# First mixture of experts on one core: activation on pairs of pieces, masks one unit later, normalization applied by ScalarE

## The chip, the cores and the metric

One core of a Trainium2 chip runs the whole kernel. The metric is the device time of one execution in microseconds (us); the profile of one execution is taken beside it. Five engines work in parallel, each through its own list of instructions in order: TensorE (PE, with its weight loads PEld), VectorE (DVE), ScalarE (ACT), GpSimd (POOL) and SyncE (SP, which here only issues transfers). They wait for one another through counting semaphores.

## The reference, cut to what matters

A decoder of two layers over 16 sequences of 128 tokens with 256 features. Each layer has two attentions (the first layer: a gated recurrence and a masked attention) and a mixture of experts, and after each of the six comes `x = layernorm(x + sublayer(x))`. The change touches the third of the six, the first mixture of experts: 8 experts of inner width 64, of which each token uses the best two by router score.

```python
x1 = ragged_dot(xb, w1b, gs); x3 = ragged_dot(xb, w3b, gs)      # bf16
h = silu(x1) * x3
routed = ragged_dot(h, w2b, gs)
out = sum over the token's two experts of score * routed
x = layernorm(x + out)
```

## The kernel before, in words

The phases are named A to F, one for each sublayer. Phase C is the first mixture of experts. It computes all 8 experts for all tokens (8 x 64 = 512 hidden features) and masks the hidden values for each of the two choices before the product with `w2`. A **unit** is two sequences (256 tokens), so there are NU = 8 units; the 512 hidden features are N0 = 4 **pieces** of 128. For each piece f of unit t:

1. PE `c_up` writes both products (w1 and w3, four matmuls) into one PSUM bank of 512 columns; there is one bank for each piece.
2. ACT `c_up` (L824) copies the bank as bf16 into `up0`.
3. ACT `c_exp` (L832), DVE `c_den` (L1262: plus one, and a cap), ACT `c_ln` (L838), ACT `c_sig` (L846) make the sigmoid as exp(-ln(1 + exp(-x))); DVE `c_act` (L1271) multiplies it with x, POOL `c_prod` (L627) with the other product.
4. PE `c_mask` (L1783, two matmuls) spreads the 0/1 choice of each token over the piece's lanes, for choice 0 and choice 1. There are two mask banks for the four pieces.
5. DVE `c_hid` (L1282) multiplies mask and product into `hid0`, 512 columns, and so frees the mask bank.

For each unit and each choice r, PE `c_down` (L1796, eight matmuls) sums the four pieces through `w2`, ACT `c_round` (L866) copies the result as bf16, DVE `c_sub` (L1293, called `add` in the pipeline) adds it, scaled by the token's score, to x. Then the layer norm: DVE `stats` (L1077 to L1083) gives mean and variance, POOL `inverse_root` (L597) the inverse root, DVE `apply` (L1090) writes the normalized rows into `X`.

Each engine's list is made by `pipelined(engine, n, stages)`: in **turn** s it emits, in the order of the list, each stage with its lag for unit s - lag. The order inside a turn is therefore fixed by hand, for each engine. `behind(f, k, stage)` gives the stage for the piece k places before f, in this turn or the one before. Buffers for exp, den, sig, act, prod and ln hold two pieces and are used in turn. Before the change the orders of turn s are (piece, and unit in brackets):

- PE: up0[s], mask2[s-1], down0[s-2], up1[s], mask3[s-1], down1[s-2], up2[s], mask0[s], up3[s], mask1[s]
- ACT: up0, ln3[s-1], exp0, sig3[s-1], up1, ln0, exp1, sig0, round[s-2], up2, ln1, exp2, sig1, up3, ln2, exp3, sig2 (unit s where nothing is said)
- DVE: den0, act3[s-1], hid2[s-1], den1, apply[s-3], act0, hid3[s-1], den2, act1, hid0, add[s-2], den3, act2, hid1, stats[s-2]
- POOL: inverse root[s-3], prod0, prod1, prod2, prod3

Behind phase C comes phase D, whose first step on PE, `xpose_unit` and `d_proj`, reads the rows of unit 0: PE transposes (L1737), ACT `evac_d` (L880), DVE `d_x_low` (L1312), then the matmuls of `d_proj` (L1606). ACT and DVE come to that work only when all of phase C in their lists is done. POOL then clears `kz` (L641, one memset of 4096 columns) and splits the keys.

Phase A already applies its norm on ACT: POOL makes `nmean` (L603) and `nbias` (L606), ACT writes the rows (L758).

Of the kernel before, what the change touches and what calls it, by code (L numbers as in the profile page):

```python
# [168 lines left out]
def decoder(nc, a, out, xg, yg, qk):  # L169
    with ExitStack() as ctx:  # L170
# [378 lines left out]
        def _(pool):  # L549
# [87 lines left out]
            pipelined(pool, NU, [(3, inverse_root("C"))] + [(0, c_prod(f)) for f in range(N0)])  # L637
# [77 lines left out]
        def _(act):  # L715
# [111 lines left out]
            def c_exp(f):  # L827
                def step(t, slot):
                    act.wait_ge(sem("C_up"), t * N0 + f + 1)
                    if f >= 2 or not (isinstance(t, int) and t < 1):  # L830
                        act.wait_ge(sem("C_den"), t * N0 + f - 1)
                    sc.activation(exp0[:, f % 2, :], up0[:, f, 0, :], ACT.Exp, scale=-1.0).then_inc(sem("C_exp"), 1)  # L832
                return step

            def c_ln(f):
                def step(t, slot):
                    act.wait_ge(sem("C_den"), t * N0 + f + 1)
                    sc.activation(ln0[:, f % 2, :], den0[:, f % 2, :], ACT.Ln).then_inc(sem("C_ln"), 1)  # L838
                return step

            def c_sig(f):
                def step(t, slot):
                    act.wait_ge(sem("C_ln"), t * N0 + f + 1)
                    if f >= 2 or not (isinstance(t, int) and t < 1):
                        act.wait_ge(sem("C_act"), t * N0 + f - 1)
                    sc.activation(sig0[:, f % 2, :], ln0[:, f % 2, :], ACT.Exp, scale=-1.0).then_inc(sem("C_sig"), 1)  # L846
# [3 lines left out]
            c_up(0)(0, 0)  # L850
            c_exp(0)(0, 0)
            route_exp()

# [13 lines left out]
            stages = []  # L867
            for f in range(N0):
                up, exp = (c_up(f), c_exp(f)) if f else (but_first(c_up(f)), but_first(c_exp(f)))
                stages += [(0, up), behind(f, 1, c_ln, N0), (0, exp), behind(f, 1, c_sig, N0)]  # L870
                if f == 1:
# [1242 lines left out]
```

## Time and profile before

| | us |
|---|---|
| time, median of 3 runs (lowest to highest) | 812.95 (812.26 to 814.93) |
| time of the profiled execution | 808.24 |
| its span | 806.5 |
| phase C, first `c_den` to the first matmul of `d_proj` | 178.44 to 262.37 |

In the page, busy time is the time an engine's instructions took, and the mean granted clock of PE (PEclk, 1.00 is 2.4 GHz, 0.50 is 1.2 GHz) stands beside each stretch. Behind an instruction in the timeline, square brackets say how long its engine was idle before it and what ended that. Start times count from the span's start. A duration is not the distance to the next start: on ACT and DVE the next instruction begins somewhat before the last one has ended.

### The profile page before, as it was taken

What the parts mean: (1) busy time and instruction counts of PE and PEld (TensorE: products, weight loads), DVE (VectorE), ACT (ScalarE), POOL (GpSimd) and SP (SyncE); (2) the same over time, 40 slices, a digit from 0 to 9 for tenths busy, and PEclk for the clock granted to TensorE, in tenths of its full rate; (3) what the DMA queues carried; (4) which work ended last, traced back from release to release, by engine and by line L of the source; (5) the groups of instructions that cost most, each with busy time, mean ns of one, the idle gap of its engine ahead of it and who ended that gap; (6) DMA issues with size and microseconds to landing.
All of it is one profiled execution on the core that took longest, in us unless ns stands there. A gap on an engine that the chain in (4) does not pass through costs nothing.

```text
span 806.5 us, 17830 instructions
## 1 busy us (share of the span) xinstructions
PE 704.8 (87%) x5074; PEld 627.8 (78%) x5075; DVE 556.4 (69%) x1498; ACT 469.1 (58%) x1179; POOL 234.6 (29%) x399
## 2 busy tenths in 40 slices
PE   6887699958864988999999999999699989999972
PEld 5886477734432988999998999999599978888872
DVE  4786387757888446777786788887566765555376
ACT  4453466538782227777776788887345545555433
POOL 3122200033334600112121121111154515555544
PEclk9999699966695899999999999999699999999996
DMA  9940000000002586656667566652025433333162
GB/s 291 355 118 0 1 1 1 0 0 1 0 1 105 154 278 203 179 162 202 190 189 207 146 192 168 160 157 74 0 84 136 144 95 98 97 99 102 45 227 79
DMA packets 66486, 95.59 MB, mean 119 GB/s; under 512 B 11391, under 2 KB 52993, under 8 KB 66305
## 3 DMA queue, kind: packets, MB, share of 16 engines
q1 hardware_dynamic: 63024, 86.51, 36.3%
q0 software_dynamic: 3408, 8.43, 2.9%
q8 instruction: 26, 0.43, 0.2%
q14 instruction: 28, 0.22, 0.1%
HBM read 62.45 MB, written 33.36 MB: 119 GB/s over the span
## 4 chain that ended last, share of the span: by engine, by line
PE 58%; issue 16%; DVE 12%; DMA 4%; POOL 3%; ACT 3%; SPq 3%; DVEq 0%; POOLq 0%; ACTq 0%
PE bank L1875 13%; PE bank L1861 7%; PE bank L1951 6%; PE bank L2017 5%; PE bank L1850 4%; PE bank L1844 3%; PE bank L2041 3%; PE bank L1968 3%; PE bank L1606 3%; PE bank L1891 2%; PE bank L2005 2%; SPq L478 1%; DMA k_D<-stage_d 1%; DVE X L1090 1%; PE bank L1640 1%
## 5 line engine op out<-in xcount | busy, mean ns | idle before, releaser
L1875 PE MATMUL bank<-f_mem,late_mem 128*128 128x68 f32 (+3 forms) x1024 | 127.9, 268 | 0.0
L1875 PEld LDWEIGHTS bank<-f_mem,late_mem 128*128 128x128 f32 x1024 | 124.5, 192 | 0.7 <-issue 0.5
L597 POOL TENSOR_TENSOR rstd<-var,power 128x2 f32<-128x2 f32 (+1 forms) x64 | 41.7, 651 | 219.4 <-DVE var L1083 208.5
L1336 DVE TENSOR_REDUCE smax<-bank 128x4 f32<-128x512 f32 x128 | 88.2, 690 | 22.3 <-PE bank L1850 20.9
L915 ACT ACTIVATE late_mem<-bank 128x512 f32<-128x512 f32 x128 | 77.7, 607 | 21.6 <-PE bank L1861 19.3
L905 ACT ACTIVATE late_mem<-bank,smax 128x128 f32<-128x128 f32 x256 | 73.8, 384 | 11.4 <-DVE smax L1336 11.4
L1861 PE MATMUL bank<-ident,late_mem 128*128 128x128 f32 x512 | 77.3, 273 | 2.9 <-ACT late_mem L905 1.6
L1850 PE MATMUL bank<-kz,qs 128*128 128x256 f32 x256 | 75.1, 376 | 0.0
L1861 PEld LDWEIGHTS bank<-ident,late_mem 128*128 128x128 f32 x512 | 59.2, 141 | 3.6 <-ACT late_mem L905 2.0
L899 ACT ACTIVATE late_mem<-late_mem 128x512 f32<-128x512 f32 x64 | 41.0, 641 | 24.1 <-DVE late_mem L1343 23.3
L1850 PEld LDWEIGHTS bank<-kz,qs 128*128 128x128 f32 x256 | 48.7, 191 | 6.1 <-issue 0.3
L1951 PE MATMUL bank<-x_hi,w_hi 128*128 128x256 f32 x176 | 51.6, 293 | 1.0 <-DVE x_lo L1400 1.0
L1951 PE MATMUL bank<-x_lo,w_hi 128*128 128x256 f32 x176 | 50.8, 288 | 0.0
L1951 PE MATMUL bank<-x_hi,w_lo 128*128 128x256 f32 x176 | 50.7, 288 | 0.0
L1844 PE MATMUL bank<-causal,identb 128*128 128x512 bf16 x128 | 48.7, 381 | 1.2 <-DVE hidden_mem L1327 1.2
L1343 DVE TENSOR_TENSOR late_mem<-bank,smax 128x512 f32<-128x512 f32 x64 | 44.3, 692 | 6.9 <-DVE smax L1336 0.5
L686 POOL DMA_INDIRECT xg<-X,idx x32 | 33.6, 1049 | 42.7 <-DMA xg<-X,idx 21.2
L698 POOL DMA_INDIRECT yg<-attn_w,dest x39 | 38.8, 995 | 20.4 <-issue 12.0
L1968 PE MATMUL bank<-w_hi,hid_hi 128*128 128x256 f32 (+1 forms) x96 | 29.9, 311 | 13.8 <-DVE hid_lo L1417 13.7
L977 ACT ACTIVATE f_mem<-bank 128x256 f32<-128x256 f32 x40 | 15.3, 384 | 40.9 <-PE bank L1951 40.7
L1407 DVE TENSOR_TENSOR f_mem<-bank,f_mem 128x256 f32<-128x256 f32 x40 | 17.0, 424 | 30.0 <-ACT f_mem L977 29.7
L627 POOL TENSOR_TENSOR late_mem<-late_mem,f_mem 128x256 bf16<-128x256 bf16 x32 | 21.4, 669 | 52.1 <-DVE late_mem L1271 52.1
(285 smaller groups left out, 2069.9 us busy)
## 6 DMA issues: line engine op xcount, KB each, us to landing
qs<-q_D SPq DMA_DIRECT2D x64, 128.0 KB, 2.7
kz<-k_D SPq DMA_DIRECT2D x128, 64.0 KB, 2.6
qs<-q_E SPq DMA_DIRECT2D x64, 128.0 KB, 2.7
kz<-k_E SPq DMA_DIRECT2D x128, 64.0 KB, 2.5
xg<-f_mem SPq DMA_DIRECT2D x1, 5031.0 KB, 22.7
late_mem<-xg SPq DMA_DIRECT2D x39, 129.0 KB, 2.1
q_D<-stage_d SPq DMA_DIRECT2D x8, 512.0 KB, 2.9
k_D<-stage_d SPq DMA_DIRECT2D x8, 512.0 KB, 4.0
```

Source lines behind the costliest of these rows:

```text
L597: gp.tensor_tensor(rstd[:, slot, 0:n], var[:, slot, 0:n], power[:, 0:n], ALU.pow).then_inc(sem("ln_rstd"), 1)
L899: sc.activation(sp[:, g, :, :], sp[:, g, :, :], ACT.Exp).then_inc(sem("core_exp"), 1)
L905: ins = sc.activation(sp[:, g, i, :], bank[g][:, i * P:(i + 1) * P], ACT.Exp, bias=smax[:, g, i:i + 1])
L915: sc.activation(spt[:, g, :, :], bank[4 + g % 2][:, :], ACT.Copy).then_inc(sem("core_pts"), 1)
L1336: ve.tensor_reduce(smax[:, g, :], v, axis=AX.X, op=ALU.max, negate=g not in SUBS).then_inc(sem("core_max"), 1)
L1343: ve.tensor_tensor(sp[:, g, :, :], v, smax[:, g, :].unsqueeze(2).to_broadcast([P, HG, P]), ALU.subtract).then_inc(sem("core_sub"), 1)
L1844: mm(bank[g][:, :], identb[:, :], causal[:, :].unsqueeze(1).to_broadcast([P, HG, P]), start=True, stop=False)
L1850: ins = mm(bank[g][:, i * D:(i + 1) * D], qs[slot][:, a_ * P:(a_ + 1) * P], kz[:, slot, :, a_ * P:(a_ + 1) * P], start=False, stop=(i == 1))
L1861: ins = nc.tensor.transpose(bank[4 + g % 2][:, i * P:(i + 1) * P], sp[:, g, i, :], ident[:, :])
L1875: ins = mm(bank[6][:, h * (DH + 1):to * (DH + 1)], spt[:, g, i, :], vf[:, slot, h:to, :].rearrange("p h d -> p (h d)"), start=True, stop=True)
L1951: ins = mm(bank[r][:, m * UT:(m + 1) * UT], w[:, lo:lo + P], x[:, t % 2, k, :], start=(n == 1), stop=(n == 3 * KC))
L1968: ins = mm(halves(6 + t % 2)[:, j, :], h[lanes, r, cols], v[lanes, w], start=(f == n == j == 0), stop=(f == NF - 1 and n == 2 and j == UB ...
```

## The change

Exp, den, ln, sig, act and prod work on a **pair** of pieces (512 columns) in place of one (256 columns): NP0 = 2 instructions of each for a unit in place of 4, with buffers of twice the size for both pairs. The masks move: PE makes all four in the turn after the unit's up products, and DVE's four `hid` follow there. The statistics move one turn later. `apply` leaves DVE: POOL gets `nmean` and `nbias` in phase C too, ACT writes the rows. The orders of turn s become (a number behind exp, den, ln, sig, act, prod is now a pair):

- PE: up0[s], mask0[s-1], down0[s-2], up1[s], mask1[s-1], down1[s-2], up2[s], mask2[s-1], up3[s], mask3[s-1]
- ACT: up0, up1, ln1[s-1], exp0, sig1[s-1], round[s-2], up2, up3, ln0, exp1, sig0, apply[s-3]
- DVE: hid0[s-1], den0, act1[s-1], hid1[s-1], stats[s-3], den1, act0, hid2[s-1], hid3[s-1], add[s-2]
- POOL: prod1[s-1], inverse root[s-3], shift[s-3], prod0

```diff
@@ POOL
-            def c_prod(f):
+            def shift(phase, base):
+                def step(t, slot):
+                    gp.tensor_tensor(nmean[:, slot, :], mv[:, slot, :, 0], minus[:, 0:UB], ALU.mult).then_inc(sem("A_minus"), 1)
+                    pool.wait_ge(sem("A_minus"), t + 1 + base)
+                    pool.wait_ge(sem("ln_rstd"), t + 1 + LN[phase])
+                    gp.tensor_tensor(nbias[:, slot, :], nmean[:, slot, :], rstd[:, slot, :], ALU.mult
+                                     ).then_inc(sem("A_shift"), 1)
+                return step
+            def c_prod(p):
                 def step(t, slot):
-                    pool.wait_ge(sem("C_act"), t * N0 + f + 1)
-                    if f >= 2 or not (isinstance(t, int) and t < 1):
-                        pool.wait_ge(sem("C_hid"), t * N0 + f - 1)
-                    gp.tensor_tensor(prod0[:, f % 2, :], act0[:, f % 2, :], up0[:, f, 1, :], ALU.mult
+                    pool.wait_ge(sem("C_act"), t * NP0 + p + 1)
+                    if not (isinstance(t, int) and t < 1):
+                        pool.wait_ge(sem("C_hid"), (t - 1) * N0 + 2 * p + 2)
+                    gp.tensor_tensor(prod0[:, p, :, :], act0[:, p, :, :], up0[:, 2 * p:2 * p + 2, 1, :], ALU.mult
                                      ).then_inc(sem("C_prod"), 1)
-            pipelined(pool, NU, [(3, inverse_root("C"))] + [(0, c_prod(f)) for f in range(N0)])
+            pipelined(pool, NU, [(1, c_prod(1)), (3, inverse_root("C")), (3, shift("C", NU)), (0, c_prod(0))])
@@ ACT
                 def step(t, slot):
                     act.wait_ge(sem("C_hx"), t * N0 + f + 1)
                     if not (isinstance(t, int) and t < 1):
-                        act.wait_ge(sem("C_prod"), (t - 1) * N0 + f + 1)
+                        act.wait_ge(sem("C_prod"), (t - 1) * NP0 + f // 2 + 1)
                     sc.activation(up0[:, f, :, :], halves(HB[f]), ACT.Copy).then_inc(sem("C_up"), 1)
+            def c_apply(t, slot):
+                act.wait_ge(sem("A_shift"), t + 1 + NU)
+                for j in range(UB):
+                    ins = sc.activation(xrow(t * UB + j), y[:, slot, j, :], ACT.Identity,
+                                        bias=nbias[:, slot, j:j + 1], scale=rstd[:, slot, j:j + 1])
+                ins.then_inc(sem("ln_x"), 1)
+            pipelined(act, NU, [(0, but_first(c_up(0))), (0, but_first(c_up(1))), (1, c_ln(1)), (0, but_first(c_exp(0))),
+                                (1, c_sig(1)), (2, c_round), (0, c_up(2)), (0, c_up(3)), (0, c_ln(0)), (0, c_exp(1)),
+                                (0, c_sig(0)), (3, c_apply)])
@@ DVE
-            add, stats, apply = layer_norm("C", c_sub, own_n=2 * UB, split=True)
+            add, stats, _ = layer_norm("C", c_sub, own_n=2 * UB, split=True)
+            pipelined(dve, NU, [(1, c_hid(0)), (0, c_den(0)), (1, c_act(1)), (1, c_hid(1)), (3, stats),
+                                (0, c_den(1)), (0, c_act(0)), (1, c_hid(2)), (1, c_hid(3)), (2, add)])
@@ PE, c_up
                     if not isinstance(t, int):
-                        pe.wait_ge(sem("C_hid"), t * N0 + f - 3)
+                        pe.wait_ge(sem("C_hid"), t * N0 + f - N0 - 1)
@@ PE
-                stages += [(0, c_up(f)), behind(f, 2, c_mask, N0)]
+                stages += [(0, c_up(f)), (1, c_mask(f))]
                 if f < 2:
                     stages.append((2, c_down(f)))
```

`c_down(r)` for unit t keeps its wait for all four `hid` of its unit, `C_hid` at (t + 1) * 4.

## Rows read from the trace of the kernel before

**Rows 1.** The page, part 1: busy time of each engine over the whole span.
```profile
PE 704.8 (87%) x5074; PEld 627.8 (78%) x5075; DVE 556.4 (69%) x1498; ACT 469.1 (58%) x1179; POOL 234.6 (29%) x399
```

**Rows 2.** Windows of phase C: busy time by engine, PEclk, DMA share, GB/s.
```profile
182.00:252.00 70.00, 55.79 (x296) 29.34 (x296) 56.00 (x173) 50.91 (x131) 24.41 (x38) 0.72 0.00 1
208.00:218.00 10.00, 9.47 (x41) 4.63 (x42) 8.08 (x26) 7.36 (x19) 3.33 (x6) 0.50 0.00 0
```

**Rows 3.** Waits in phase C, 175 to 256: us in total, times, longest.
```profile
DVE f_mem L1262 <- ACT f_mem L832: 9.1, 15, 2.0
PE bank L1767 <- DVE hidden_mem L1282: 8.6, 10, 1.7
```

**Rows 4.** Timeline of ACT: the copy of piece 0 of units 2 and 7.
```profile
188.19 0.60 ACT L824 ACTIVATE f_mem<-bank 128x512 bf16<-128x512 f32 x1
...
234.02 0.59 ACT L824 ACTIVATE f_mem<-bank 128x512 bf16<-128x512 f32 x1
```

**Rows 5.** Timeline of ACT: a copy of 512 columns and two functions of 256.
```profile
208.99 0.60 ACT L824 ACTIVATE f_mem<-bank 128x512 bf16<-128x512 f32 x1 [0.87 <-PE bank L1767]
209.48 0.41 ACT L838 ACTIVATE late_mem<-f_mem 128x256 f32<-128x256 bf16 x1
209.79 0.41 ACT L832 ACTIVATE f_mem<-f_mem 128x256 bf16<-128x256 bf16 x1
```

**Rows 6.** Timeline of DVE: act, hid and the beginning of an add.
```profile
240.68 0.29 DVE L1271 TENSOR_TENSOR late_mem<-f_mem,late_mem 128x256 bf16<-128x256 bf16 x1
240.89 0.68 DVE L1282 TENSOR_TENSOR hidden_mem<-bank,late_mem 128x512 bf16<-128x512 f32 x1
241.49 0.91 DVE L1293 SCALAR_TENSOR_TENSOR y<-hidden_mem,m,X 128x256 f32<-128x256 bf16 x2
```

**Rows 7.** Timeline of PE: a down and an up behind it, at either clock.
```profile
200.59 1.05 PE L1796 MATMUL bank<-late_mem,hidden_mem 128*128 128x256 bf16 x8
201.47 0.60 PE L1767 MATMUL bank<-up_mem,late_mem 128*128 x4
...
209.42 1.89 PE L1796 MATMUL bank<-late_mem,hidden_mem 128*128 128x256 bf16 x8
211.09 1.06 PE L1767 MATMUL bank<-up_mem,late_mem 128*128 x4
```

**Rows 8.** Groups by line and shape, whole span: busy us, mean ns | idle before.
```profile
L899 ACT ACTIVATE late_mem<-late_mem 128x512 f32<-128x512 f32 x64 | 41.0, 641 | 24.1 <-DVE late_mem L1343 23.3
...
L758 ACT ACTIVATE X<-y,nbias,rstd 128x256 f32<-128x256 f32 x8 | 4.3, 590 | 10.7 <-POOL nbias L606 10.7
...
L627 POOL TENSOR_TENSOR late_mem<-late_mem,f_mem 128x256 bf16<-128x256 bf16 x32 | 21.4, 669 | 52.1 <-DVE late_mem L1271 52.1
...
L706 POOL TENSOR_TENSOR ctx_mem<-ctx_mem,late_mem 128x512 f32<-128x512 f32 x6 | 8.1, 1351 | 7.4 <-DMA late_mem<-yg 7.4
...
L606 POOL TENSOR_TENSOR nbias<-nmean,rstd 128x2 f32<-128x2 f32 x8 | 1.6, 197 | 0.6
```

**Rows 9.** Timeline of DVE: the first den of phase C.
```profile
178.44 0.20 DVE L1262 TENSOR_SCALAR f_mem<-f_mem 128x256 bf16<-128x256 bf16 x1
```

**Rows 10.** Timeline of the end of phase C: DVE, POOL and PE.
```profile
248.04 0.68 DVE L1282 TENSOR_TENSOR hidden_mem<-bank,late_mem 128x512 bf16<-128x512 f32 x1
...
254.98 0.75 DVE L1077 BATCH_NORM_STATS2 st<-y 128x6 f32<-128x256 f32 x2
...
256.05 0.17 DVE L1083 TENSOR_SCALAR var<-mv 128x2 f32<-128x2 f32 x1
256.30 0.69 POOL L597 TENSOR_TENSOR rstd<-var,power 128x2 f32<-128x2 f32 x1 [3.83 <-DVE var L1083]
256.93 3.51 POOL L641 MEMSET kz<- 128x4096 f32 x1
257.03 4.60 DVE L1090 TENSOR_SCALAR X<-y,mv,rstd 128x256 f32<-128x256 f32 x2 [0.81 <-POOL rstd L597]
...
262.37 0.55 PE L1606 MATMUL bank<-xp_hi,wd_hi 128*128 128x256 f32 x1 [7.32 <-DVE xp_lo L1312]
```

More of the change, by code:

```diff
@@ L40 @@
 N0 = E * F0 // P
+NP0 = N0 // 2
 NF = 6
@@ L338, in decoder @@
         up0 = part(small_mem, 0, [P, N0, 2, UT], BF16)
-        exp0, den0 = (part(small_mem, (4 + k) * UT, [P, 2, UT], BF16) for k in range(2))
-        sig0, act0, prod0 = (part(late_mem, 2048 + k * UT, [P, 2, UT], BF16) for k in range(3))
+        exp0, den0 = (part(f_mem, 2112 + k * 2 * UT, [P, 2, 2, UT], BF16) for k in range(2))
+        sig0, act0 = (part(late_mem, 2048 + k * 2 * UT, [P, 2, 2, UT], BF16) for k in range(2))
+        prod0 = part(late_mem, 6400, [P, 2, 2, UT], BF16)
         xt1 = part(small_mem, 4 * KC * P, [P, 2, KC, P])
-        ln0 = part(late_mem, 2048 + 3 * UT, [P, 2, UT])
+        ln0 = part(early_mem, 0, [P, 2, 2, UT])
         qs = (rounded("qs0", "late_mem", 6400, [P, NP * P]), rounded("qs1", "f_mem", 3136, [P, NP * P]))
@@ L822, in step, with c_exp @@
                     if not (isinstance(t, int) and t < 1):
-                        act.wait_ge(sem("C_prod"), (t - 1) * N0 + f + 1)
+                        act.wait_ge(sem("C_prod"), (t - 1) * NP0 + f // 2 + 1)
                     sc.activation(up0[:, f, :, :], halves(HB[f]), ACT.Copy).then_inc(sem("C_up"), 1)
                 return step
-            def c_exp(f):
+            def c_exp(p):
                 def step(t, slot):
[L829 to L832, printed above, removed]
+                    act.wait_ge(sem("C_up"), t * N0 + 2 * p + 2)
+                    if not (isinstance(t, int) and t < 1):
+                        act.wait_ge(sem("C_den"), (t - 1) * NP0 + p + 1)
+                    sc.activation(exp0[:, p, :, :], up0[:, 2 * p:2 * p + 2, 0, :], ACT.Exp, scale=-1.0).then_inc(sem("C_exp"), 1)
@@ L833, in c_exp, with c_ln, c_sig @@
                 return step
-            def c_ln(f):
+            def c_ln(p):
                 def step(t, slot):
-                    act.wait_ge(sem("C_den"), t * N0 + f + 1)
-                    sc.activation(ln0[:, f % 2, :], den0[:, f % 2, :], ACT.Ln).then_inc(sem("C_ln"), 1)
+                    act.wait_ge(sem("C_den"), t * NP0 + p + 1)
+                    sc.activation(ln0[:, p, :, :], den0[:, p, :, :], ACT.Ln).then_inc(sem("C_ln"), 1)
                 return step
-            def c_sig(f):
+            def c_sig(p):
@@ L842, in step @@
                 def step(t, slot):
[L843 to L846, printed above, removed]
+                    act.wait_ge(sem("C_ln"), t * NP0 + p + 1)
+                    if not (isinstance(t, int) and t < 1):
+                        act.wait_ge(sem("C_act"), (t - 1) * NP0 + p + 1)
@@ L847, in c_sig @@
+                    sc.activation(sig0[:, p, :, :], ln0[:, p, :, :], ACT.Exp, scale=-1.0).then_inc(sem("C_sig"), 1)
                 return step
             sc.preload_act_table_set("natural_log_exp_and_others")
-            c_up(0)(0, 0)
-            c_exp(0)(0, 0)
-            route_exp()
             def but_first(step):
@@ L858, in but_first @@
                 return other
+            for f in range(2):
+                c_up(f)(0, 0)
+            c_exp(0)(0, 0)
+            route_exp()
             def c_round(t, slot):
@@ L866, in c_round @@
                     sc.activation(down0[:, slot, r, :], bank[4 + r][:, :], ACT.Copy).then_inc(sem("C_dnb"), 1)
[L867 to L871, printed above, removed]
-                    stages.append((2, c_round))
-            pipelined(act, NU, stages)
+            def c_apply(t, slot):
[7 more added lines that the diff above has]
+                                (0, c_sig(0)), (3, c_apply)])
             def evac_d(t, slot):
@@ L1074, in stats @@
                         add(t, slot)
+                    own.n, own.t = own_n, t
                     own.sync()
@@ L1287, in c_sub @@
             def c_sub(t, slot, own):
+                if not (isinstance(t, int) and t < 2):
+                    dve.wait_ge(sem("ln_x"), t - 1 + LN["C"])
                 for r, m in ((0, m1), (1, m2)):
@@ L1296, in c_sub @@
                         own.sync()
-            add, stats, apply = layer_norm("C", c_sub, own_n=2 * UB, split=True)
-            stages = []
-            for f in range(N0):
-                stages += [(0, c_den(f)), behind(f, 1, c_act, N0), behind(f, 2, c_hid, N0)]
-                if f in (2, 3):
-                    stages.append((2, add if f == 2 else stats))
-            stages.insert(4, (3, apply))
-            pipelined(dve, NU, stages)
+            add, stats, _ = layer_norm("C", c_sub, own_n=2 * UB, split=True)
+            pipelined(dve, NU, [(1, c_hid(0)), (0, c_den(0)), (1, c_act(1)), (1, c_hid(1)), (3, stats),
+                                (0, c_den(1)), (0, c_act(0)), (1, c_hid(2)), (1, c_hid(3)), (2, add)])
             def d_x_low(t, slot):
```

31 lines of the change are left out of this document (13 added, 18 removed).

## The prediction

> **What bounds the kernel now.** I read the page first: over the span PE is busy 87% [rows 1], but phase C is a tenth of the span and is judged by its own rows. The windows of its middle show no full engine: in 70 us PE has 55.8 busy, DVE 56.0, ACT 50.9, POOL 24.4 [rows 2]. PE's figure depends on its clock: the mean granted clock is 0.72, so it stood at 2.4 GHz for some 44% of the time and at 1.2 GHz for the rest (0.5 + 0.5 x 0.44), and where it stood at 1.2 GHz throughout, PE was busy 9.47 of 10 us. Then the waits: DVE's den waits for ACT's exp 9.1 us in all, PE's up products wait for DVE's hid 8.6 us [rows 3]. So the phase is a ring of short waits between PE, ACT and DVE, and what counts is the longest path around that ring in one turn. The copy of piece 0 of units 2 and 7 gives the turn: (234.02 - 188.19) / 5 = 9.17 us [rows 4]. Last I read the end of the phase in the timeline: from the last hid (248.04 + 0.68) to the first matmul of phase D (262.37) pass 13.65 us [rows 10], and phase D, the same code before and after, hangs on that matmul. So the sum is made for one point: when does `d_proj` begin?
>
> **Prices of single instructions.** From start to start ACT takes 0.49 us for the copy of 512 columns and 0.31 for 256 columns (durations 0.60, 0.41) [rows 5]. An exp of 512 columns took 0.64 us (f32) against 0.41 for 256; I take 0.62, and 0.52 to the next start. Bounds: 0.60, as a copy, and 0.64 [rows 5, 8]. DVE's act of 256 columns takes 0.29 and 0.21 to the next start; a second 256 columns cost nothing at least and 0.29 at most, I take 0.13: hid, not packed, needs 0.68 for 512, and a fixed part is paid once. So 0.42, and 0.34 to the next start. Hid takes 0.68, next start after 0.60; an add takes twice 0.91 and a short wait, 1.92 in all [rows 6]. POOL's product takes 0.67 for 256 columns. For 512 it lies between 0.67 and 1.35 (the f32 tensor-tensor of 512); I take 1.20, near the upper row because that is the same operation on the same engine [rows 8]. Crossing from one engine to another costs 0.08 (256.22 to 256.30) and 0.04 (256.99 to 257.03) [rows 10]; I take 0.07.
>
> **Work of each engine.** ACT per turn: 12 x 0.31 = 3.7 becomes 6 x 0.52 = 3.12, and apply adds 2 x 0.49 = 0.98 (duration 0.59, [rows 8]): +0.4. DVE: 4 acts at 0.21 become 2 at 0.34 (-0.16), 4 dens become 2 (about -0.2), apply leaves (-0.7): about -1.0. POOL: 4 x 0.67 becomes 2 x 1.20 (-0.3) and nmean, nbias add 0.4. PE: the same 40 matmuls. None of this decides unless the ring lets it.
>
> **The ring after the change.** Three orders matter. DVE now makes hid3[s-2] near the end of turn s-1, behind act0[s-1], where it used to be done early. PE's down0[s-2] needs it and stands in front of up1[s]. And on ACT ln1[s-1], exp0[s] and sig1[s-1] stand behind the copy up1[s]. Behind sig1[s-1] come act1[s-1] and prod1[s-1], for which the copy up2[s] waits because it overwrites what the product reads; and ln0, exp1, sig0[s] stand behind that. DVE makes hid3[s-1] only behind act0[s], which waits for sig0[s]. That closes the ring, from sig0 to sig0 of the next unit, at 2.4 GHz:
>
> act0 0.34, hid2 0.60, hid3 0.68 = 1.62; down0 0.88 and up1 0.60 = 1.48 [rows 7]; ACT up1 0.49, ln1 0.52, exp0 0.52, sig1 0.62 = 2.15; act1 0.42 and prod1 1.20 = 1.62; ACT up2 0.49, up3 0.49, ln0 0.52, exp1 0.52, sig0 0.62 = 2.64; six crossings 0.42. Sum 9.93 us.
>
> At 1.2 GHz PE is not yet free when hid3 is there: up0 (0.86) and mask0 (0.43, four and two matmuls at 0.21) start when hid2 is done at 1.16, then down0 1.67 and up1 1.06 [rows 7] end at 5.18 in place of 3.24 or so: +1.92, a ring of 11.85. With the clock's present share, 0.44 x 9.93 + 0.56 x 11.85 = 11.0 us. Hidden in the ring are add (1.92), hid0, den0 and stats on DVE, round and apply on ACT, and the two small POOL operations: DVE is through with add, hid0 and den0 at 4.4, sig1 comes at 5.2 or later; ACT's round ends before prod1; apply ends at 1.1 and up0 has to wait for prod0 until 1.83 anyway. So the copy up0 has the apply in front of it for nothing.
>
> **Where it begins.** The first den starts at 178.44 [rows 9], for 512 columns about 0.29; ln0, exp1, sig0 behind it end at 180.46. Turn 1 has no down; its ring goes through both products: 1.83 (act0, prod0, three crossings) + 2.64 + 1.83 + 2.64 = 8.94. Six turns with downs follow: sig0 of unit 7 ends at 180.46 + 8.94 + 6 x 11.0 = 255.4.
>
> **The end.** From there DVE runs act0, hid2, hid3, add[5], hid0, act1, hid1, stats[5] (1.24, from 254.98 to 256.22), hid2, hid3 of unit 7: done after 7.6 [rows 10]. Add[6] and stats[6] last until 10.8; the two downs (3.6 us at 1.2 GHz) and the second rounding let the last add end at 13.0, the last variance at 14.3. Then POOL's three operations, 0.69 + 2 x 0.20 and crossings, 1.2; two applies 0.98, `evac_d` behind them in ACT's list 0.60, `d_x_low` 0.68 and two crossings: `d_proj` starts after 18.0. Measured from the last hid that is 10.4 us, against 13.65 before: this end is 3.2 us shorter. Most of that is one stall that goes: the last apply took 4.60 us for two instructions, because POOL's memset (256.93, 3.51 us) ran beside it [rows 10]. ACT's apply of phase A took 0.59 an instruction [rows 8].
>
> The Trainium skill, page "SBUF — State Buffer", section "SBUF: two separate sides", says that VectorE and GpSimd share a port pair as an exclusive lock while ScalarE has its own port; by that rule the stall is gone wholly, as in my sum, and the trace agrees with its 4.60 us.
>
> **Sum.** 255.4 + 18.0 = 273.4 against 262.37: +11.0 us, thus 819.3 against the profiled execution's 808.24, and 812.95 + 11.0 = 824.0 against the median, which lies 4.7 us above the profiled one. Break-even is a ring of (262.37 - 18.0 - 180.46 - 8.94) / 6 = 9.16 us.
>
> **Rivals.**
> 1. *PE stays at 2.4 GHz* where down0 and up1 run. Ring 9.93, end 17.7: 180.46 + 8.94 + 59.6 + 17.7 = 266.7, +4.3 us, 817.3. For it: the phase had long stretches at that level. Against it: PE will idle more, 40 matmuls in a longer turn.
> 2. *PE is at 1.2 GHz for each of them*: 6 x 11.85, +16, 829. For it: the pair comes right behind PE's longest idle time in the turn.
> 3. *Up1 is never late* (down0 passes early enough). The ring is that of turn 1, 8.94: 180.46 + 7 x 8.94 + 17.7 = 260.7, -1.6 us, no change that can be told. Against it: the wait for all four hid stands in the code.
> 4. *Faster: work, not the ring, sets the turn.* Fewer, longer instructions relieve DVE, the busiest engine beside PE at 8 us of 10 [rows 2], by 1.0 us a turn. 9.17 becomes 8.2: 6 x -1.0 and -3.2 at the end give -9, 804. It decides when the ring takes under 9.16, that is, if the long ring of waits found above is broken somewhere by 1.9 us. Against it: even without down0 in it, the ring is 8.94.
>
> Beside rival 4 stands a rule of the Trainium skill that speaks for the change: page "VectorE: DVE Perf Modes", section "Rules for kernel authors", tells to keep the number of operations small, since each pays a fixed cost. The trace agrees on the fixed cost (0.41 us for 256 columns, 0.64 for 512), but no row says that a saving on DVE shortens a turn here.
>
> **How the numbers follow.** Forecast, ring 10.3 to 11.6: 0.60. Rival 1: 0.12, rival 2: 0.10, rival 3: 0.08, rival 4: 0.10. A measurement here tells 0.3%, 2.4 us, from no change. Slower: 0.82, same 0.08, faster 0.10. If the product takes 0.67 the result is 0.53 x 7 = 3.7 us less, with 1.35 it is 1 us more; both stay inside the clock's bounds. The range leaves out rivals 3 and 4 and what lies beyond rival 2: 813.5 to 829.5.
>
> **What would show it.** ACT's copy of piece 0 should return every 10 to 12 us in units 2 to 7, and some 9 us in turn 1; ACT should wait for PE before up1 (1 to 3 us) and for POOL before up2 (0.5 to 1 us); PE should wait for DVE's hid before down0; DVE should be idle 3 us or more of a turn, waiting for exp and sig; the applies at 0.59 us, none near 4 us; 10 to 11 us from the last hid to `d_proj`; phase D and all behind it unchanged in length. A turn of 9 us or less, or up1 ready before ACT asks for it, would make the prediction wrong.

## The result, and the profile after

The changed kernel takes 830.02 us (median of 4 runs, 829.3 to 832.41) against 813.25 us (4 runs, 812.26 to 814.93): a ratio of 1.0209, 95% interval 1.0181 to 1.0237. It is 16.8 us slower where +11.0 was forecast, and lies 0.5 us beyond the upper end of the range. The direction and the ring of waits were right; what the low clock does to that ring was put too small.

First the page of the changed kernel, part 1. Against [rows 1] DVE is 12 us less busy, and PE 9 us more with the same number of matmuls.

```profile
PE 713.3 (86%) x5074; PEld 633.9 (76%) x5075; DVE 544.2 (66%) x1450; ACT 472.2 (57%) x1147; POOL 234.6 (28%) x399
```

Then the starts of ACT's sig of the first pair in the timeline, for units 0, 1 and 7. They give the turns: 8.82 us for turn 1, and (264.02 - 193.94) / 6 = 11.68 us for the six behind it (11.06, 11.67, 12.24, 11.74, 12.23, 11.14). Forecast were 8.94 and 11.0.

```profile
185.12 0.61 ACT L852 ACTIVATE late_mem<-late_mem 128x512 bf16<-128x512 f32 x1
...
193.94 0.63 ACT L852 ACTIVATE late_mem<-late_mem 128x512 bf16<-128x512 f32 x1
...
264.02 0.63 ACT L852 ACTIVATE late_mem<-late_mem 128x512 bf16<-128x512 f32 x1
```

The same starts in the kernel before (sig of piece 0, units 0, 1 and 7) give 5.58 us for turn 1 and (237.88 - 184.88) / 6 = 8.83 us for the six behind it:

```profile
179.30 0.40 ACT L846 ACTIVATE late_mem<-late_mem 128x256 bf16<-128x256 f32 x1
...
184.88 0.41 ACT L846 ACTIVATE late_mem<-late_mem 128x256 bf16<-128x256 f32 x1
...
237.88 0.40 ACT L846 ACTIVATE late_mem<-late_mem 128x256 bf16<-128x256 f32 x1
```

So of the changed kernel's longer phase C, 17.1 us lie in the six turns (70.1 less 53.0) and 3.2 us in turn 1, and the stretch behind the start of the last sig0 gives 5.8 us back (18.7 instead of 24.5).

The waits between 174 and 300 us (total, times, longest) name the ring. PE waits 19.2 us for hid ahead of the up products, against 8.6 in [rows 3], and 12.8 more ahead of the masks; DVE's den waits 34.4 for exp, against 9.1; ACT's copy waits for PE and, new, for POOL's product. (The changed kernel also lets DVE's add wait for ACT's apply of two units earlier; no row of these waits shows DVE held there.)

```profile
DVE f_mem L1273 <- ACT f_mem L838: 34.4, 15, 3.6
ACT f_mem L830 <- PE bank L1774: 23.1, 13, 2.5
PE bank L1774 <- DVE hidden_mem L1293: 19.2, 8, 4.1
...
PE bank L1790 <- DVE hidden_mem L1293: 12.8, 7, 4.1
ACT f_mem L830 <- POOL late_mem L633: 10.8, 9, 1.8
```

One turn in the timeline, from act0[4] to sig0[5], with the engine's idle time in brackets. It is the forecast ring, link by link:

```profile
217.33 0.43 DVE L1282 TENSOR_TENSOR late_mem<-f_mem,late_mem 128x512 bf16<-128x512 bf16 x1 [0.22 <-ACT late_mem L852]
217.68 1.28 DVE L1293 TENSOR_TENSOR hidden_mem<-bank,late_mem 128x512 bf16<-128x512 f32 x2
...
218.50 1.03 PE L1774 MATMUL bank<-up_mem,late_mem 128*128 x4 [3.57 <-DVE hidden_mem L1293]
...
219.47 0.60 PE L1790 MATMUL bank<-f_mem,hidden_mem 16*128 x2
...
220.00 1.89 PE L1803 MATMUL bank<-late_mem,hidden_mem 128*128 128x256 bf16 x8
...
221.68 1.06 PE L1774 MATMUL bank<-up_mem,late_mem 128*128 x4
...
222.78 0.60 ACT L830 ACTIVATE f_mem<-bank 128x512 bf16<-128x512 f32 x1 [2.51 <-PE bank L1774]
...
224.31 0.62 ACT L852 ACTIVATE late_mem<-late_mem 128x512 bf16<-128x512 f32 x1
...
225.05 0.42 DVE L1282 TENSOR_TENSOR late_mem<-f_mem,late_mem 128x512 bf16<-128x512 bf16 x1 [0.31 <-ACT late_mem L852]
...
225.65 1.15 POOL L633 TENSOR_TENSOR late_mem<-late_mem,f_mem 128x512 bf16<-128x512 bf16 x1 [6.66 <-DVE late_mem L1282]
...
226.90 1.08 ACT L830 ACTIVATE f_mem<-bank 128x512 bf16<-128x512 f32 x2 [1.00 <-POOL late_mem L633]
...
228.91 0.63 ACT L852 ACTIVATE late_mem<-late_mem 128x512 bf16<-128x512 f32 x1
```

The windows of this turn (length, PE, PEld, DVE, ACT, POOL busy, PEclk, DMA share, GB/s) show what the forecast had not seen. PE is wholly idle in 216 to 218, and up0, mask0, down0 and up1, which run from 218.5 to 222.7, all run at 0.50, the level of 1.2 GHz. The clock is back at 1.00 only when they are done, and stays there while ACT waits for POOL's product instead. (In the turn before this one it rose a little earlier, for up1 already, 0.68 us instead of 1.06; that turn took 11.67 us, this one 12.24.) The mean over 76 us of such turns is 0.75, higher than the 0.72 of [rows 2].

```profile
186.00:262.00 76.00, 47.79 (x256) 25.01 (x254) 38.83 (x101) 44.68 (x85) 20.29 (x26) 0.75 0.00 0
...
216.00:218.00 2.00, 0.00 (x0) 0.00 (x0) 0.96 (x3) 2.00 (x5) 0.37 (x3) 0.75 0.00 0
218.00:220.00 2.00, 1.50 (x6) 0.60 (x7) 1.97 (x5) 0.61 (x2) 0.99 (x1) 0.50 0.00 0
220.00:222.00 2.00, 2.00 (x11) 1.44 (x11) 1.26 (x3) 0.26 (x1) 0.00 (x0) 0.50 0.00 0
222.00:224.00 2.00, 2.00 (x11) 0.92 (x10) 0.00 (x0) 1.22 (x3) 0.00 (x0) 0.54 0.03 8
224.00:226.00 2.00, 1.30 (x11) 0.73 (x9) 1.25 (x4) 1.90 (x4) 0.35 (x1) 1.00 0.02 4
```

This is a turn of PE's loop, for units 3 to 6. The turns of units 2 and 7 are written out, and there up0 has no wait for hid and is done long before. What is left behind the idle time, mask0, down0 and up1, runs at the low level there too, and these turns took 11.06 and 11.14 us. Unit 7:

```profile
254.62 0.60 PE L1790 MATMUL bank<-f_mem,hidden_mem 16*128 16x256 bf16 x2 [3.04 <-DVE hidden_mem L1293]
255.22 1.89 PE L1803 MATMUL bank<-late_mem,hidden_mem 128*128 128x256 bf16 x8
256.90 1.06 PE L1774 MATMUL bank<-up_mem,late_mem 128*128 128x256 bf16 x4
```

Last the end of the phase in the timeline, to be held against [rows 10]. The last hid ends at 272.53 and `d_proj` starts at 282.75, 10.2 us later (forecast 10.4, before 13.65). POOL's memset still runs beside the last apply, but the apply is now ACT's and takes its usual 1.09 us for two instructions.

```profile
271.24 1.29 DVE L1293 TENSOR_TENSOR hidden_mem<-bank,late_mem 128x512 bf16<-128x512 f32 x2 [0.45 <-PE bank L1790]
...
280.20 3.51 POOL L647 MEMSET kz<- 128x4096 f32 x1
280.31 1.09 ACT L878 ACTIVATE X<-y,nbias,rstd 128x256 f32<-128x256 f32 x2 [2.29 <-POOL nbias L610]
...
282.75 0.55 PE L1613 MATMUL bank<-xp_hi,wd_hi 128*128 128x256 f32 x1 [3.89 <-DVE xp_lo L1319]
```

Phase C (first den, 183.76, to `d_proj`) is thus 98.99 us long against 83.93. This length is given for every run below, because what lies around it scatters by some us from one execution to the next. Each of the two kernels was profiled once more. The kernel before (e5):

> The kernel before once more, for a second profile: how far do the phases that nothing touches wander from one execution to the next? In the first pair of profiles the changed kernel's phase C is 15.1 us longer, but its first den starts 5.3 us later and all behind phase C takes 3.8 us longer. Theory: both are scatter of one execution (the profiled one of before was 4.7 us under its median); then this profile has its first den nearer 181 and phase C at 83 to 86 us. Rival: the untouched phases of the kernel before are always faster; then den starts at 178.4 again and the rest takes 544.

It took 814.88 us, with a phase C of 85.0. The changed kernel (e6):

> The changed kernel once more, for a second profile, as the run before. Theory, scatter: phase C 98 to 100 us again, the turns 11 to 12.3 us with up0, mask0, down0 and up1 at 1.2 GHz in each of PE's loop turns; the rest within 4 us of 548, in either direction. Rival: the low clock in front of down0 was chance in the first profile; then some turns are near 10 us here and phase C is under 95.

It took 829.41 us, with a phase C of 99.07 and turns within 0.05 us of the first profile's. So the change lengthens phase C by 14.6 us (99.03 less 84.47, the means of two profiles each) of the 16.8.

### The profile page after: what moved, and what is told of

The parts are those of the page before. It is cut to its first block, busy times and chain, and to the rows that moved or that the text cites. A ratio compares the mean times of both kernels' runs of the same rounds, so it can differ in the third digit from the quotient of the medians.

```text
span 830.7 us, 17676 instructions
## 1 busy us (share of the span) xinstructions
PE 713.3 (86%) x5074; PEld 633.9 (76%) x5075; DVE 544.2 (66%) x1450; ACT 472.2 (57%) x1147; POOL 234.6 (28%) x399
## 4 chain that ended last, share of the span: by engine, by line
PE 56%; issue 15%; DVE 12%; ACT 5%; DMA 4%; SPq 3%; POOL 3%; ACTq 0%; DVEq 0%; POOLq 0%
PE bank L1882 12%; PE bank L1868 6%; PE bank L2024 5%; PE bank L1958 5%; PE bank L1857 3%; PE bank L1613 3%; PE bank L2048 3%; PE bank L1851 3%; PE bank L1975 3%; PE bank L1803 2%; PE bank L1898 2%; SPq L480 2%; PE bank L1647 2%; PE bank L2012 2%; DMA k_D<-stage_d 1%
## 5 line engine op out<-in xcount | busy, mean ns | idle before, releaser
L915 ACT ACTIVATE late_mem<-bank,smax 128x128 f32<-128x128 f32 x256 | 73.5, 383 | 11.3 <-DVE smax L1343 11.3
L1774 PE MATMUL bank<-up_mem,late_mem 128*128 (+1 forms) x128 | 26.0, 347 | 20.1 <-DVE hidden_mem L1293 19.2
L633 POOL TENSOR_TENSOR late_mem<-late_mem,f_mem 128x512 bf16<-128x512 bf16 x16 | 18.4, 1152 | 68.6 <-DVE late_mem L1282 68.6
```

The costliest lines, as they stand in the source:

```text
L915: ins = sc.activation(sp[:, g, i, :], bank[g][:, i * P:(i + 1) * P], ACT.Exp, bias=smax[:, g, i:i + 1])
```

## The experiments

The turns, phase C and time, side by side. The ratio is that to the kernel before as it ran beside each kernel, with medians of 810.5 to 813.3 us, so kernels are compared by the ratio and not by the time:

| kernel | mean of the six turns behind turn 1 | phase C | time | ratio, 95% interval |
|---|---|---|---|---|
| before | 8.83, 9.01 | 83.9, 85.0 | 813.25 | 1 |
| changed kernel | 11.68 | 99.0 | 830.02 | 1.0209 (1.0181 to 1.0237) |
| e1 filler in the loop | 10.57 | 92.4 | 827.22 | 1.0212 (1.017 to 1.0254) |
| e12 filler in each turn | 10.43 | 91.4 | 822.43 | 1.0136 (1.011 to 1.0162) |
| e2 up1 ahead of down0 | 10.47 | 92.1 | 825.09 | 1.0178 (1.0126 to 1.0231) |
| e3 all ups first | 8.95 | 82.6 | 815.63 | 1.0046 (1.0019 to 1.0072) |
| e7 hid2, hid3 early | 9.06 | 82.4 | 813.24 | 1.0019 (0.9998 to 1.0041) |
| e11 the same, apply on DVE | 9.08 | 85.4 | 814.74 | 1.0025 (0.9997 to 1.0052) |
| e8 e3, products on DVE | 8.82 | 80.8 | 809.83 | 0.9981 (0.9955 to 1.0008) |
| e10 e8, last apply early | 8.63 | 76.7 | 806.97 | 0.9936 (0.9913 to 0.9959) |
| e4 before, apply on ACT | 9.59 | 84.6 | 813.3 | 1.0028 (1.0012 to 1.0044) |
| e9 before, memset late | 8.53 | 78.3 | 808.54 | 0.9955 (0.9932 to 0.9979) |

**Is it the clock of that stretch (e1, e12)?** The changed kernel with 20 matmuls more, which nothing reads, ahead of up0's wait in the turns that run as a loop, so that PE is busy where it was idle:

```diff
+                    if not isinstance(t, int) and f == 0:
+                        for _ in range(5):
...
+                                    mm(halves(HB[f])[:, o, :], w[:, c, f * P:(f + 1) * P], XTB[:, c, bass.ds(t * UT, UT)],
...
                     if not isinstance(t, int):
                         pe.wait_ge(sem("C_hid"), t * N0 + f - N0 - 1)
```

> The changed kernel, with PE's four matmuls of up0 repeated five more times (20 matmuls, same bank, same result) in front of up0's wait for hid, where PE idles 3.6 us in each turn of the loop. Theory, clock: the ring itself is 9.9 us at 2.4 GHz; the turns take 11.7 us because the idle time before down0 lets the clock fall and up0, mask0, down0, up1 run at 1.2 GHz. Then the clock holds, the four turns of PE's loop fall to 10.0 to 10.4 us, and the kernel gets faster by 5 to 7 us than the changed one, about 824, although it does more work. Rival, order alone: the turn is set by waits that do not depend on the clock; then nothing is gained, and the filler, 2.2 to 4.3 us in a gap of 3.6, leaves 830 or costs some us.

The filled turns took 10.07 to 10.55 us. The first and the last of the six, which the edit doesn't reach, stayed at 11.06 and 11.15. In the timeline the critical stretch now runs in 0.61, 1.05 and 0.60 us instead of 1.03, 1.89 and 1.06:

```profile
202.85 0.61 PE L1780 MATMUL bank<-up_mem,late_mem 128*128 x4 [1.70 <-DVE hidden_mem L1293]
...
203.72 1.05 PE L1809 MATMUL bank<-late_mem,hidden_mem 128*128 128x256 bf16 x8
...
204.60 0.60 PE L1780 MATMUL bank<-up_mem,late_mem 128*128 x4
```

and its windows show the full clock where the changed kernel had 0.50:

```profile
202.00:204.00 2.00, 1.15 (x9) 0.68 (x10) 2.00 (x5) 0.48 (x1) 1.15 (x1) 1.00 0.00 0
204.00:206.00 2.00, 2.00 (x18) 1.44 (x17) 1.67 (x4) 0.88 (x3) 0.00 (x0) 1.00 0.00 0
```

The filler does not keep the clock up throughout. In the next turn it fell while the filler itself ran, and was back at 1.00 for the critical stretch:

```profile
210.00:212.00 2.00, 2.00 (x11) 1.45 (x10) 0.45 (x2) 2.00 (x5) 0.72 (x3) 0.50 0.00 0
214.00:216.00 2.00, 2.00 (x18) 1.38 (x17) 1.74 (x4) 0.96 (x2) 0.00 (x0) 1.00 0.00 0
```

There the slowed filler took 4.02 us and held up0 back until 213.23, some 0.3 us behind the end of hid2; so what the filler gives back is, if anything, less than what the low clock costs.

Phase C shrank by 6.6 us. The whole kernel did not show it: 827 us where some 824 were expected, and a ratio of 1.0212 beside the changed kernel's 1.0209, with an interval of 3.4 us to either side. So the filler was put in every turn from unit 2 on (`if f == 0 and not (isinstance(t, int) and t < 2)`) and timed in six runs:

> The changed kernel with 20 matmuls that nothing reads ahead of up0 in every turn from unit 2 on, the turns written out at either end included. Theory (the clock of the stretch up0 to up1 is what lengthens the turns behind turn 1, and the time it gives back reaches the end of the kernel): turn 1 stays 8.8, all five following turns 10 to 10.6, phase C 90.5 to 92.5 us against 99.0, and the kernel 6 to 8 us faster than the changed kernel, a ratio to the kernel before of 1.011 to 1.014. Rival (the phases behind give the gain back, as four runs of the first filler kernel left possible): the same phase C, and a ratio of 1.018 or more.

Turns of 10.77, 10.07, 10.58, 10.34, 10.47 and 10.34, phase C 91.4, and a ratio of 1.0136, as expected. By the two ratios that is 5.9 us under the changed kernel, give or take 3 us; by phase C it is 7.6. In some of these turns up0 still began at the low level (0.65 to 0.95 us), but down0 and up1 ran at 1.05 and 0.60 in all. So the low clock of that stretch costs about 6 to 7.6 us. The rest of the loss is the ring itself.

**Is it down0 in front of up1 (e2, e3)?** PE's order becomes up0, up1, down0, mask0, mask1, down1, up2, mask2, up3, mask3, and up0 and up1 no longer wait for hid:

```diff
-                    if not isinstance(t, int):
+                    if not isinstance(t, int) and f >= 2:
                         pe.wait_ge(sem("C_hid"), t * N0 + f - N0 - 1)
...
-                stages += [(0, c_up(f)), (1, c_mask(f))]
+            pipelined(pe, NU, [(0, c_up(0)), (0, c_up(1)), (2, c_down(0)), (1, c_mask(0)), (1, c_mask(1)), (2, c_down(1)),
+                               (0, c_up(2)), (1, c_mask(2)), (0, c_up(3)), (1, c_mask(3))])
```

> The changed kernel with one change of PE's order: up1 ahead of mask0 and down0 (up0, up1, down0, mask0, mask1, down1, up2, mask2, up3, mask3), and up0 and up1 without their wait for hid. Theory, ring through hid3, down0, up1: ACT has up1 when it asks; what is left is the ring through both products, 8.9 us, with up3 late by up to 1.6 us where PE is at 1.2 GHz: turns of 9.3 to 10.5, kernel 816 to 823. Rival, the two products set the turn and PE is only late beside them: no gain beyond 2 us, 828 to 830.

Turns of 10.94, 10.77, 10.56, 8.99, 10.97 and 10.57: the ring had moved, not gone. Down0, still held by hid3, now stood in front of mask0, down1 and up2, again at the low clock:

```profile
203.18 1.88 PE L1803 MATMUL bank<-late_mem,hidden_mem 128*128 128x256 bf16 x8 [2.59 <-DVE hidden_mem L1293]
205.00 1.03 PE L1790 MATMUL bank<-f_mem,hidden_mem 16*128 x4
205.96 1.89 PE L1803 MATMUL bank<-late_mem,hidden_mem 128*128 128x256 bf16 x8
...
209.16 0.80 PE L1774 MATMUL bank<-up_mem,late_mem 128*128 x4
```

The turn of 8.99 us is the only one of the six whose down0 ran at 2.4 GHz:

```profile
224.51 1.05 PE L1803 MATMUL bank<-late_mem,hidden_mem 128*128 128x256 bf16 x8 [2.69 <-DVE hidden_mem L1293]
```

With the low clock in it this ring takes 10.6 to 11.0 us, without it no more than the ring through the products. The kernel, at 825.09 us, landed between the theory's 816 to 823 and the rival's 828 to 830.

With all four ups ahead of every down (the waits for hid stand at the masks, and turns are written out):

```diff
+            stages = [(0, c_up(f)) for f in range(N0)]
             for f in range(N0):
-                stages += [(0, c_up(f)), (1, c_mask(f))]
+                stages.append((1, c_mask(f)))
```

> The changed kernel with all four up products of unit s at the head of PE's turn, ahead of all masks and downs, with the waits for hid on the masks (PE's turns written out, no loop). Theory: no up product is ever late at either clock; the ring through both products remains, turns of 8.9 to 9.2 us, kernel 813 to 816, about the kernel before. Rival, ACT or DVE busy time or PE's clock sets the turn: turns stay above 10 us, kernel over 820; second rival, the products do not bind: turns near 8 us, kernel 807.

Every turn took 8.82 to 9.06 us, about the length of turn 1, and the time was within what was expected. The first row shows ACT's copy waiting for the product; from 180 to 262 us it waits 14.2 us for products and in no row for PE. The second row shows that the clock in 60 us of the phase was 0.78, little above the changed kernel's 0.75. Down0 still ran at either level, at 1.05 us in a turn of 8.83 and at 1.89 in the next, of 8.84: with no down ahead of an up product the low clock no longer lengthens a turn.

```profile
220.77 1.08 ACT L830 ACTIVATE f_mem<-bank 128x512 bf16<-128x512 f32 x2 [0.90 <-POOL late_mem L633]
```

```profile
186.00:246.00 60.00, 41.58 (x244) 22.81 (x243) 38.07 (x103) 46.19 (x90) 20.16 (x28) 0.78 0.00 1
```

**Or is it hid3 behind act0 (e7)?** The same link cut at its other end: PE as in the change, but DVE makes hid2 and hid3 before den1 and act0:

```diff
 pipelined(dve, NU, [(1, c_hid(0)), (0, c_den(0)), (1, c_act(1)), (1, c_hid(1)), (3, stats),
-                    (0, c_den(1)), (0, c_act(0)), (1, c_hid(2)), (1, c_hid(3)), (2, add)])
+                    (1, c_hid(2)), (1, c_hid(3)), (0, c_den(1)), (0, c_act(0)), (2, add)])
```

> The changed kernel with one change of DVE's order: hid2 and hid3 of unit s-1 stand ahead of den1 and act0 of unit s, not behind them; PE's order as in the changed kernel. Theory, the ring closes through act0 in front of hid3: now hid3 no longer waits for sig0, down0 finds it done, and the ring through both products remains: turns of 8.9 to 9.3 us, phase C 82 to 86, kernel as e3 (about +4 us against before). Rival, PE's order is the cause (up1 behind mask0 and down0, whoever makes hid): turns stay at 11 or more.

Turns of 8.84 to 9.15, phase C 82.4, ratio 1.0019, as expected: this one place in DVE's list held nearly the whole loss. In its timeline PE still has idle time and even low-clock turns (up0 takes 1.03 us at 223.55), but ACT's copy of up0 and up1 at 225.85 waits for POOL's product, so PE is early.

```profile
223.55 1.03 PE L1774 MATMUL bank<-up_mem,late_mem 128*128 x4 [2.05 <-DVE hidden_mem L1293]
...
225.85 1.09 ACT L830 ACTIVATE f_mem<-bank 128x512 bf16<-128x512 f32 x2 [0.89 <-POOL late_mem L633]
```

**What is the ring that is left (e8)?** It goes through both products on POOL, 1.15 us each. In the kernel with all ups first the products went to DVE, right behind act (0.43 us there):

```diff
+                    ve.tensor_tensor(prod0[:, p, :, :], act0[:, p, :, :], up0[:, 2 * p:2 * p + 2, 1, :], ALU.mult
...
-            pipelined(pool, NU, [(1, c_prod(1)), (3, inverse_root("C")), (3, shift("C", NU)), (0, c_prod(0))])
+            pipelined(pool, NU, [(3, inverse_root("C")), (3, shift("C", NU))])
...
+            pipelined(dve, NU, [(1, c_hid(0)), (0, c_den(0)), (1, c_act(1)), (1, c_prod(1)), (1, c_hid(1)), (3, stats),
+                                (0, c_den(1)), (0, c_act(0)), (0, c_prod(0)), (1, c_hid(2)), (1, c_hid(3)), (2, add)])
```

> The kernel of e3 with the products made by DVE, each right behind its act (POOL keeps inverse root, nmean, nbias). Theory: the ring of 8.9 us goes twice through a product on POOL (1.15 us and two crossings); on DVE it is 0.42 and a wait of 0.05, while DVE's work grows by 0.7 a turn: turns of 7.9 to 8.4 us, phase C 76 to 79, kernel about 4 us faster than e3, that is, within 1 us of before. Rival, DVE becomes the bound and the order no longer fits: turns of 8.8 or more, no gain over e3.

Turn 1 fell from 8.82 to 7.28 us, so that ring was the product's. The others fell by 0.1 us only: they took 8.31 to 9.58, and in them PE waits for hid (14.5 us in all from 180 to 262) and ACT's rounds wait for PE (13.8). So the turns of 7.9 to 8.4 that were expected did not come; another ring holds them, which was not taken apart. The ratio, 0.9981, lies some 5 us under that of e3, where about 4 were expected; but only 1.8 us of that lie in phase C, and the kernel can't be told from the kernel before.

**Apply on ACT alone (e4), and apply back on DVE (e11).** The kernel before, with apply on ACT behind the rounds:

> The kernel before with only the last part of the change: the normalization of phase C applied by ScalarE (POOL makes nmean and nbias), placed on ACT behind the rounding; pieces, masks and statistics as before. Theory: the stall of the last apply beside POOL's memset goes (4.6 us for two instructions become 1.1, less 0.5 for the longer chain through POOL: about -3 us), and DVE is relieved of 0.65 us a turn, of which up to half shows: kernel 807 to 811. Rival, ACT becomes late: 0.98 us a turn more on ACT, in a ring of short waits, takes back more than the end gives: 813 to 818.

```diff
                 if f == 1:
-                    stages.append((2, c_round))
+                    stages += [(2, c_round), (3, c_apply)]
```

Phase C 84.6 and ratio 1.0028 (1.0012 to 1.0044): no gain but some 2 us lost, as the rival said. The stall at the end went, but the six turns behind turn 1 grew from 8.83 and 9.01 (two profiles) to 9.59 us. DVE's den waits 18.9 us for ACT's exp from 180 to 262 us, against 8.3 in the kernel before from 180 to 256, so ACT's list is on the path here. Back on DVE, in the kernel with the early hids (the one edit: `(3, apply)` at the end of DVE's list, no `nmean` and `nbias` on POOL):

> As the run with the last two hids ahead of den and act (813.24 us, ratio 1.0019), with the apply back on VectorE behind its turn's work. Theory (a turn is set by the ring of waits and not by VectorE's sum of work): the loop's turns stay at about 9.1 us; at the end the apply runs beside POOL's memset again and takes 4 to 5 us, so phase C is about 85 us and the kernel 2 to 3 us slower than that run (ratio about 1.005). Rival: VectorE's 0.7 us more per turn lengthens every turn to 9.6 us or more, phase C 88 us or more.

The turns stayed (9.08 against 9.06), so DVE had the room. The last apply again met the memset, and phase C grew by 3.0 us:

```profile
262.40 3.88 DVE L1101 TENSOR_SCALAR X<-y,mv,rstd 128x256 f32<-128x256 f32 x2 [0.80 <-POOL rstd L599]
```

The ratio rose by 0.0006 only; its interval of 0.005 cannot confirm 3 us nor exclude them.

**The stall by itself (e9).** The kernel before, with POOL's memset held back until the last apply is through (in this kernel it is DVE that makes it, not ScalarE as the expectation has it):

```diff
             pool.wait_ge(sem("C_o"), 2 * NU)
+            pool.wait_ge(sem("ln_x"), LN["D"])
             gp.memset(kz
```

> The kernel before, with the one edit that POOL's clearing of the keys' buffer waits until ScalarE has taken the last unit's ln. Theory (the last unit's VectorE apply of 4.60 us was held up by POOL's memset running beside it, the other seven took about 0.7 us): the last apply takes 0.7 to 0.8 us, phase C about 80 to 81 us instead of 84 to 85, and the kernel is 3 to 4 us faster than the kernel before, so a gain of that size needs nothing of the change. Rival: what delays the last apply is not the memset, or the memset, now later, delays the first part of phase D by as much: no difference.

```profile
257.00 0.74 DVE L1091 TENSOR_SCALAR X<-y,mv,rstd 128x256 f32<-128x256 f32 x2 [0.81 <-POOL rstd L597]
...
257.86 3.51 POOL L642 MEMSET kz<- 128x4096 f32 x1 [0.89 <-DVE X L1091]
```

The apply took 0.74 instead of 4.60 us, the stretch from the last sig0 to `d_proj` 20.6 instead of 24.5, and the kernel became faster: 0.9955. (Its phase C is shorter by some 2 us more, in turns that the edit doesn't touch: the last six took 51.2 us here and 53.0 and 54.0 in the two profiles of before. The mean granted clock over these six turns was 0.84, 0.73 and 0.66, so the lower clock goes with the longer turns.) From the end of the last hid to `d_proj` pass 9.8 us, against 13.65 in the kernel before and 10.2 in the changed one: what the change gained at this end is had by one wait. The Trainium skill, page "SBUF — State Buffer", section "SBUF: two separate sides", gives VectorE and GpSimd one port pair that one of them holds alone, and ScalarE its own: the trace agrees, with 3.88 and 4.60 us on DVE beside the memset, 0.74 apart from it, and 1.09 on ACT beside it.

**A version that beats both (e10).** The kernel with the products on DVE, and the last unit's apply taken out of phase C's list on ACT, where phase D's `evac_d` stood behind it, and put behind the first two `evac_d`, ahead of the first high halves (`d_high`):

```diff
+            def last_apply(t, slot):
+                if isinstance(t, int) and t == 1:
+                    c_apply(NU - 1, (NU - 1) % 2)
-            pipelined(act, NU, [(0, evac_d), (1, d_high(0)), (1, d_high(1))])
+            pipelined(act, NU, [(0, evac_d), (0, last_apply), (1, d_high(0)), (1, d_high(1))])
```

> As the run with all four ups first and the products on VectorE (809.83 us, ratio 0.998), with the last unit's apply put ahead of the first high halves in ScalarE's order at the end. Theory (the end of the phase is set by the chain last hid, statistics, apply, first matmul of phase D): phase C about 78 to 79 us instead of 80.8, the kernel 2 to 3 us less than that run, ratio to the kernel before 0.994 to 0.996. Rival: phase D waits for something else (its high halves), and the time stays at a ratio of 0.998.

`d_proj` of unit 0 needs nothing of unit 7, and it now starts before unit 7's rows are written:

```profile
257.15 0.55 PE L1620 MATMUL bank<-xp_hi,wd_hi 128*128 128x256 f32 x1 [0.96 <-DVE xp_lo L1326]
```

```profile
257.64 1.09 ACT L875 ACTIVATE X<-y,nbias,rstd 128x256 f32<-128x256 f32 x2 [0.82 <-POOL nbias L610]
```

Phase C is 76.7 us, 4.1 under the kernel with the products on DVE; 2.9 of them lie behind the end of the last sig0 (15.7 instead of 18.6 us), and the others in turns that the edit doesn't touch. The time is 806.97 us, ratio 0.9936 (0.9913 to 0.9959). That is clear of the kernel before, but not of e9 with its one wait (0.9932 to 0.9979).

## Why the prediction came out too low

- **The start and turn 1** held: from the first den to the end of sig0[0] 1.97 us (forecast 2.02), turn 1 8.82 (8.94).
- **The prices** held: exp, ln and sig 0.62 to 0.63 (0.62), act 0.42 to 0.43 (0.42), the product 1.15 (1.20), apply 0.59 (0.59).
- **The ring** is the forecast one, and cutting it at either end (e3, e7) brings the turn back to 8.95 and 9.06, close to the 8.94 of rival 3. Its orders were read rightly, and most of what was to show it came: ACT's waits for PE (2.0 to 2.5 us before up1) and mostly for POOL before up2 (0.8 to 1.0), the applies at 0.59 us, the 10.2 us from the last hid. But PE's wait for hid stands ahead of up0 or mask0 and never ahead of down0 in the six turns, since at 1.2 GHz hid3 is done before PE comes to down0; and whether all behind phase C kept its length stays open.
- **The end** held: from sig0[7]'s end to `d_proj` 18.1 us (18.0). **The stall** that goes is the memset's, shown by e9.
- **The step that failed** is the term "With the clock's present share, 0.44 x 9.93 + 0.56 x 11.85 = 11.0 us"; the mean turn measured 11.68, and 6 x 0.68 = 4.1 us of the 6.0 between 824.0 and 830.0. Two things are in it. The two rings are longer than worked out: 12.24 against 11.85 in the slowest turns, of which 0.2 us are up0 and mask0 (1.50 us from start to start, not 1.29) and the rest mostly crossings of 0.10 to 0.18 us between ACT, DVE and POOL, where 0.07 stood; and 10.07 against 9.93 in the fastest filled turn, as up0 and mask0 delay down0 a little at 2.4 GHz too. With these ends the old share gives 0.44 x 10.07 + 0.56 x 12.24 = 11.3, so that accounts for some 0.3 of the 0.68. The other 0.4 is the share: it was taken as the phase's mean, as if the clock were drawn anew for each matmul. It is not. The turn itself makes the idle time, the idle time stands right before up0, and the low level falls on down0 in each of the six turns, not in 0.56 of them. That the mean stayed at 11.68 and did not reach 12.24 has two reasons in the rows: up1 was back at 1.00 in every second turn of the loop (11.67 and 11.74 against 12.24 and 12.23), and in the two written-out turns up0 did not stand ahead of mask0 (11.06 and 11.14). The forecast had put up0 into the low ring of all six. Rival 2 had named just this ("the pair comes right behind PE's longest idle time in the turn") and gave 829; it should have been the forecast, and the 0.10 that it got was the misjudgement. That its 829 is so near is luck in part: its 16 us lie in phase C alone, where the runs show 14.6.
- **Outside phase C** some 2 us remain (16.8 less 14.6). From `d_proj` to the end of ACT's last rows of the output the two profiles of the kernel before took 539.3 and 540.1 us, those of the changed kernel 543.1 and 543.6; but the kernel of e9, whose turns are ordered as before, took 543.9, and the other kernels 540.9 to 547.3 (e1 546.6, e3 545.0, e7 541.3). Whether the change costs anything there stays open. Open too is why e3, with a phase C shorter than that of before, is slower by its ratio.
- **Turn 1** is in the forecast's sum at 8.94, but it was not held against the kernel before, where it takes 5.58 us. The 3.2 us more are about what the end gives back from the last hid (3.4). So even with the ring through down0 cut (e3, e7) the ratios show no gain.
- **The fixed cost** that the prediction took from 0.41 and 0.64 us is read from rows of ScalarE, while the page it names is about VectorE. VectorE's own act shows one too, 0.29 us for 256 columns and 0.43 for 512; as the prediction said, no row makes a shorter turn of it.
- **Rival 4**, that work on DVE sets the turn, did not come: the turns grew with DVE less busy, and e11 put 0.7 us a turn back on it without lengthening one. **Rival 1** priced what e12 made by force: its ring of 9.93 measured 10.07 to 10.77.

## What to carry to other kernels

Where engines wait for each other in a ring, count the ring and not the work of an engine, and look in each list for the one instruction that stands behind a wait it doesn't need: here moving two instructions of DVE ahead of two others gave back nearly all of the 16.8 us. Take a clock not from the mean of a phase but from the stretch on the path, and ask what the engine did just before it. When a large rearrangement shows a gain at one end, test whether a single wait brings the same gain alone, as the late memset did.

## What the runs showed of the hardware

- The granted clock fell in step with the turn: 3.6 to 4.1 us without a matmul, then the critical stretch at 0.50 (but for up1 in each second turn), then 1.00, in every turn of the loop, though the mean over the six turns had risen, to 0.79 from 0.73 and 0.66 in the two profiles of before. With matmuls that nothing reads in the idle time down0 and up1 ran at 1.00, and the kernel was faster (e12); the low level was not gone but fell on the filler (0.50 in 210 to 212 of e1). The Trainium skill, page "TensorE: Matmul & The Clock Gate", section "HAM oscillation — how this bites in real kernels", tells that bursts of matmuls with waits between them are throttled and that PE is best kept busy; the trace agrees, and adds that the place of the burst decides: e3 and e7 had a mean clock of 0.78 from 186 to 246 us, and their turns stayed at about 9 us.
- A bf16 product of 512 columns took 1.15 us on POOL and 0.43 on DVE (e8). The same product of 256 columns took 0.67 on POOL [rows 8], so twice the columns cost 1.7 times as much there.
